# Six-layer local-attention kernel: the first loads in another order with semaphores of their own, and the local stage's first buffers filled while the causal stage ends

## The reference, cut to what matters

```python
mod = (_silu(c) @ wmod).reshape(8, 6, 1, -1)
sa, ca, ga, sb, cb, gb = (mod[:, i] for i in range(6))      # ga, gb kept at least 0.25 from zero
h = _layernorm(x) * (1 + ca) + sa
x = x + ga * attn(h, Wq, Wk, Wv, Wo, bo)                    # 16 heads of 64, causal
h = _layernorm(x) * (1 + cb) + sb
x = x + gb * ffn(h)                                         # what follows, six times over
...
for i in range(6):
    x = attn_layer(shift_tokens(x), Wqkv[i], q_scale[i], k_scale[i], Wo[i]) + x    # windows of 32 tokens, rotary
    x = ffn_layer(shift_tokens(x), ln_g[i], ln_b[i], W1[i], b1[i], W2[i], b2[i]) + x
```

## Time and profile before

| what | us |
|---|---|
| median of 3 runs | 4071.61 |
| lowest and highest of the 3 | 4069.26, 4075.61 |
| time of the profiled execution | 4063.49 |
| span of the profiled execution (first to last record) | 4061.4 |
| TensorE busy in it | 3807.5 |
| VectorE, ScalarE, GpSimd busy | 3026.9, 2350.1, 2311.4 |

### The profile page before, as it was taken

The page is one execution under the profiler, slowest core; times in us unless marked ns, Lnnn a source line. Parts: engine busy times, 40 slices in busy tenths (PEclk is TensorE's granted clock), DMA queues, the critical chain, the costliest instruction groups (busy, mean ns, idle before and its releaser), DMA issues.

```text
span 4061.4 us, 162148 instructions
## 1 busy us (share of the span) xinstructions
PE 3807.5 (94%) x72308; PEld 2145.7 (53%) x72308; DVE 3026.9 (75%) x3509; ACT 2350.1 (58%) x2850; POOL 2311.4 (57%) x1892
## 2 busy tenths in 40 slices
PE   7999999779999999999999999999899999999996
PEld 3555555445555555554555555555555555555553
DVE  6878777667777777776777777777777777777774
ACT  4555565546565656565656565565566566656553
POOL 3554454366565656665666656665556565666661
PEclk9999999889999999999999999999999999999998
DMA  1000000144444444443444444444444444454442
GB/s 54 4 4 4 4 4 4 38 103 98 108 98 105 102 113 108 110 107 90 107 114 100 104 97 113 107 104 98 101 114 98 106 99 105 104 115 96 110 103 80
DMA packets 162062, 348.69 MB, mean 86 GB/s; under 512 B 32606, under 2 KB 41948, under 8 KB 155100
## 3 DMA queue, kind: packets, MB, share of 16 engines
q1 hardware_dynamic: 161372, 338.32, 35.7%
HBM read 24.24 MB, written 4.19 MB: 7 GB/s over the span
## 4 chain that ended last, share of the span: by engine, by line
PE 45%; issue 2%; DMA 2%; DVE 2%; ACT 1%; SPq 1%; ACTq 0%; DVEq 0%
PE psB L632 22%; PE psA L632 17%; DMA vev<-vo 2%; PE psB L710 2%; PE psA L684 2%; PE psB L684 1%; ACT pb L937 1%; PE psA L710 1%; SPq L452 1%; SPq L468 0%; DMA kf<-h 0%; SPq L470 0%; DVE h L1163 0%; DVE wvtl L1115 0%; DVE ts L1155 0%
## 5 line engine op out<-in xcount | busy, mean ns | idle before, releaser
L1263 POOL TENSOR_TENSOR sq<-sq 128x512 f32<-128x512 f32 x384 | 490.2, 1295 | 469.5 <-ACT sq L907 468.9
L1258 POOL TENSOR_TENSOR h<-h,ts 128x512 f32<-128x512 f32 x384 | 489.9, 1276 | 210.5 <-DVE ts L1155 210.5
L1239 POOL TENSOR_TENSOR pt<-wk,pt 128x1024 f16<-128x1024 f32 (+3 forms) x256 | 367.7, 1454 | 399.8 <-DVE pt L1096 322.1
L1259 POOL TENSOR_TENSOR h<-h,ts 128x512 f32<-128x512 f32 x384 | 490.6, 1277 | 0.0
L907 ACT ACTIVATE sq<-psA 128x1024 f32<-128x1024 f32 x240 | 245.8, 1024 | 168.1 <-PE psA L632 168.1
L1147 DVE TENSOR_TENSOR h<-psA,t_rot 128x1024 f32<-128x1024 f32 x240 | 293.0, 1221 | 46.0 <-ACT sq L907 20.3
L632 PE MATMUL psB<-vev,ptb 64*32 64x65 f32 x9216 | 244.5, 225 | 55.9 <-ACT pb L937 36.9
L1155 DVE TENSOR_TENSOR ts<-psA,t_rot 128x1024 f32<-128x1024 f32 x240 | 291.4, 1214 | 3.1 <-POOL h L1259 3.1
L632 PEld LDWEIGHTS psB<-vev,ptb 64*32 64x32 f32 x9216 | 194.4, 106 | 173.1 <-issue 98.4
L1273 POOL TENSOR_SCALAR f_a<-f_a 128x512 f32<-128x512 f32 x48 | 31.2, 650 | 404.5 <-DVE f_a L1203 404.5
L1163 DVE TENSOR_TENSOR h<-h,psB 128x1024 f32<-128x1024 f32 x192 | 229.5, 1217 | 42.3 <-PE psB L632 40.2
(11 more groups left out here) (332 smaller groups left out, 10640.6 us busy)
## 6 DMA issues: line engine op xcount, KB each, us to landing
qf<-h SPq DMA_DIRECT2D x768, 136.0 KB
kf<-h SPq DMA_DIRECT2D x768, 136.0 KB
vev<-vo SPq DMA_DIRECT2D x192, 260.0 KB, 4.1
vev<-vo SPq DMA_DIRECT2D x192, 227.5 KB, 4.5
stage<-wqk SPq DMA_DIRECT2D x12, 512.0 KB, 4.8
stage<-wvl SPq DMA_DIRECT2D x12, 256.0 KB, 5.4
stage<-wof SPq DMA_DIRECT2D x6, 512.0 KB, 4.6
xb<-xt SPq DMA_DIRECT2D x8, 256.0 KB, 7.2
```

Source lines behind the costliest of these rows:

```text
L1239: e.tensor_tensor(pt[g][pr][:, :, 1, o:o + w], wk[(slot_of(s)[0] - 1) % SLOTS][:, :, 0:w], pt[g][pr][:, :, 0, o:o + w], ALU.subtract).then ...
L1258: e.tensor_tensor(halves_of(h, 0), halves_of(h, 0), t[1], ALU.subtract)
L1259: e.tensor_tensor(halves_of(h, 1), halves_of(h, 1), t[0], ALU.add).then_inc(ended["ad"])
L1263: e.tensor_tensor(sqb[c][:, 0, :], sqb[c][:, 0, :], sqb[c][:, 1, :], ALU.add).then_inc(ended["qa"])
```

## The change

The loads at the start are issued in another order and count on more semaphores (`s_ct`, `s_first`, `s_wa` for each weight). ScalarE's exponential waits for `ct` alone. The splitting of the causal weights is cut into three steps that stand at places inside batch 0, the first product with q and k weights waits for two of the three, and VectorE's work on the masks stands behind batch 0's layernorm, with a semaphore `s_masks`. TensorE waits for x of batch 0 only, and for the rest at batch 1.

The early buffers are allocated in another order, so that `stage`, `t_tab` and `xs0` lie over `ot0` (last read by `c_op` of batch 6), `wq` and `wvt` over `w16`, `xs1` and `n_s` over `h160` and `ht0`, and `t_rot` over `pt1`. SyncE loads `stage` and `t_tab` after `c_op` of batch 6. Each engine does its first local steps inside the end of the causal walk, and TensorE waits for the four PSUM tiles to come free instead of for `s_xk`.

```diff
+        ot0 = sb("ot0", [128, 8, S], F32, early)
+        w16 = [sb(f"w16{z}", [128, 3, 1024], F16, early) for z in "hl"]
+        h160 = [sb(f"h160{z}", [128, S], F16, early) for z in "hl"]
+        ht0 = sb("ht0", [128, S], F32, early)
+        pt1 = [sb(f"pt1{i}", [128, 2, 2, 8 * 160], F16, early) for i in range(2)]
...
+        stage = sb("stage", [128, 1536])
+        t_tab = sb("t_tab", [128, 4, S])
+        xs0 = [sb(f"xs0{z}", [128, S], F16) for z in "hl"]
...
         def sync(e):
-            for o, i in ((t_mats[:, :], mats), (st_masks[:, :], masks), (st_left[:, :], left), (t_vec[:, :], vecs),
-                         (t_ct[:, 0, :], ct)):
+            e.dma_start(t_ct[:, 0, :], ct).then_inc(s_ct, 16)
+            e.dma_start(t_wmod[:, :], wmod).then_inc(s_wm, 16)
+            e.dma_start(t_mats[:, :], mats).then_inc(s_first, 16)
+            e.dma_start(xb[:, 0, 0:S], xt[0]).then_inc(s_first, 16)
...
+                    if b == NB - 2:
+                        e.wait_ge(*full(("c_op", b)))
+                        heads_of(e, 0, 0)
+                        e.dma_start(flat(t_tab), tab).then_inc(s_tab, 16)
+                        e.dma_start(t_scl[:, :, :], scl).then_inc(s_tab, 16)
             for n in range(2):
                 e.wait_ge(s_xk[n], 4)
-            e.dma_start(flat(t_tab), tab).then_inc(s_tab, 16)
-            e.dma_start(t_scl[:, :, :], scl).then_inc(s_tab, 16)
-            heads_of(e, 0, 0)
             feed_of(e, 0)
...
         def tensor(e):
-            e.wait_ge(s_x, 128)
+            e.wait_ge(s_first, 32)
...
+                    elif b == 1:
+                        e.wait_ge(s_x, 16 * (NB - 1))
...
-                    e.wait_ge(s_w16, 3)
+                    e.wait_ge(s_w16, 2)
...
-            for n in range(2):
-                e.wait_ge(s_xk[n], 4)
+            for c in range(2):
+                for i in range(2):
+                    e.wait_ge(s_free[c][i], max(n for a, z, n in use.values() if (a, z) == (c, i)) + 1)
             local_tensor(e)
...
         def scalar(e):
+            e.wait_ge(s_ct, 16)
+            e.activation(t_ct[:, 1, :], t_ct[:, 0, :], ACT.Exp, scale=-1.0).then_inc(s_actc)
             e.wait_ge(s_pads, 1)
...
+                if s == last_of("c_v", "c_qk", "c_sc"):
+                    e.wait_ge(s_xk[0], 1)
+                    local_scalar(e, scalar_walk[:2])
+                if s == last_of("c_ot"):
+                    for at in ((1, 1, 0), (1, 1, 1)):
+                        e.wait_ge(*full(("c_va", NB - 1) + at))
+                    local_scalar(e, scalar_walk[2:3])
             for n in range(2):
                 e.wait_ge(s_xk[n], 4)
-            local_scalar(e)
+            local_scalar(e, scalar_walk[3:])
...
         def vector(e):
+                        if b == 0:
+                            weight_low(1)
+                            e.wait_ge(s_const, 48)
+                            e.tensor_copy(t_masks[:, :], st_masks[:, :])
+                            e.tensor_copy(flat(t_sel), st_left[:, :]).then_inc(s_masks)
+                            weight_low(2)
...
+                if s == last_of("c_va"):
+                    e.wait_ge(*full(last_of("c_v", "c_qk")))
+                    weights_low(e, -2)
             local_vector(e)
...
         def gpsimd(e):
+            local_gpsimd(e, gpsimd_walk[:1])
             for n in range(2):
                 e.wait_ge(s_xk[n], 4)
-            local_gpsimd(e)
+            local_gpsimd(e, gpsimd_walk[1:])
```

More of the change, by code:

```diff
@@ L267, in program @@
         oq = [sb(f"oq{n}", [128, 4, 256], F32, early) for n in range(2)]
-        ot = [sb(f"ot{n}", [128, 8, S], F32, early) for n in range(2)]
         wbig = flat(ot[0])[:, 0:3 * 1024]
@@ L276, in program @@
         early.close()
+        stage = sb("stage", [128, 1536])
+        t_tab = sb("t_tab", [128, 4, S])
+        xs0 = [sb(f"xs0{z}", [128, S], F16) for z in "hl"]
         wq = [sb(f"wq{z}", [128, 2, 2, 2, 2, 128], F16) for z in "hl"]
         wvt = [sb(f"wvt{z}", [128, 2, 2, 256], F16) for z in "hl"]
-        stage = sb("stage", [128, 1536])
-        xs = [[sb(f"xs{n}{z}", [128, S], F16) for z in "hl"] for n in range(2)]
+        xs = [xs0, [sb(f"xs1{z}", [128, S], F16) for z in "hl"]]
+        n_s = sb("n_s", [128, S])
+        t_rot = sb("t_rot", [128, 2, 2, 2, S])
         wo2 = [sb(f"wo{z}", [128, 8, 128], F16) for z in "hl"]
@@ L287, in program @@
         b1s = sb("b1s", [128, 6])
-        t_tab = sb("t_tab", [128, 4, S])
-        t_rot = sb("t_rot", [128, 2, 2, 2, S])
         hb = [sb(f"h{n}", [128, 2, WK]) for n in range(HN)]
@@ L296, in program @@
         sqb = [sb(f"sq{n}", [128, 2, S]) for n in range(4)]
-        n_s, n_r, n_a = (sb("n_" + x, [128, S]) for x in ("s", "r", "a"))
+        n_r, n_a = (sb("n_" + x, [128, S]) for x in "ra")
         vo = [sb(f"vo{n}", [128, 8, 4, 65]) for n in range(2)]
@@ L321, in program @@
         s_full, s_free = [sems(f"s_full{c}", 2) for c in range(2)], [sems(f"s_free{c}", 2) for c in range(2)]
-        s_const, s_x, s_wa, s_wo, s_wm, s_w1, s_w2, s_tab, s_stage, s_x1r = (
-            sem("s_" + n) for n in ("const", "x", "wa", "wo", "wm", "w1", "w2", "tab", "stage", "x1r"))
+        s_wa = sems("s_wa", 3)
+        s_const, s_first, s_ct, s_x, s_wo, s_wm, s_w1, s_w2, s_tab, s_stage, s_x1r = (
+            sem("s_" + n) for n in ("const", "first", "ct", "x", "wo", "wm", "w1", "w2", "tab", "stage", "x1r"))
         s_dm = sems("s_dm", 4)
@@ L328, in program @@
         s_out = sem("s_out")
-        s_pads, s_chain, s_silu, s_mod, s_actc, s_z = (sem("s_" + n) for n in ("pads", "chain", "silu", "mod", "actc", "z"))
+        s_masks, s_pads, s_chain, s_silu, s_mod, s_actc, s_z = (sem("s_" + n) for n in ("masks", "pads", "chain", "silu", "mod", "actc", "z"))
         s_lnq, s_lnl, s_lnr, s_lnn = (sems("s_" + n, 2) for n in ("lnq", "lnl", "lnr", "lnn"))
@@ L357, in both, with last_of @@
             return tile(key).rearrange("p (x s) -> p x s", x=2)[:, :, 0:w]
+        def last_of(*kinds):
+            return [s for s in causal if s[0] in kinds][-1]
         def full(key):
@@ L417, in sync @@
         def sync(e):
[L418 to L426 removed]
+            e.dma_start(t_ct[:, 0, :], ct).then_inc(s_ct, 16)
+            e.dma_start(t_wmod[:, :], wmod).then_inc(s_wm, 16)
+            e.dma_start(t_mats[:, :], mats).then_inc(s_first, 16)
+            e.dma_start(xb[:, 0, 0:S], xt[0]).then_inc(s_first, 16)
+            e.dma_start(t_vec[:, :], vecs).then_inc(s_const, 16)
+            for n, w in enumerate((wqa, wka)):
+                e.dma_start(wbig[:, 1024 * n:1024 * n + 1024], w).then_inc(s_wa[n], 16)
+            for o, i in ((st_masks[:, :], masks), (st_left[:, :], left)):
+                e.dma_start(o, i).then_inc(s_const, 16)
+            e.dma_start(wbig[:, 2048:3072], wva).then_inc(s_wa[2], 16)
+            for b in range(1, NB):
                 e.dma_start(xb[:, b, 0:S], xt[b]).then_inc(s_x, 16)
@@ L866, in weights_high, with local_scalar @@
             e.activation(flat(wvt[0][:, half]), stage[:, 1024:1536], ACT.Copy, scale=WS).then_inc(ended["wh"])
-        def local_scalar(e):
+        def local_scalar(e, steps):
             tables = "natural_log_exp_and_others"
-            for s in scalar_walk:
+            for s in steps:
                 kind, v = s[:2]
@@ L1031, in vector, with weight_low @@
                 chained(e.tensor_tensor(g, t_ct[:, 0, :], t_ct[:, 2, :], ALU.mult))
-            for i in range(3):
+            def weight_low(i):
                 e.wait_ge(s_w16h, i + 1)
@@ L1125, in local_vector @@
             e.memset(vev.rearrange("p c r d -> p (c r d)"), 0.0).then_inc(s_init)
-            for s in vector_walk:
+            for s in vector_walk[1:]:
                 kind, v = s[:2]
```

34 lines of the change are left out of this document (16 added, 18 removed).

## The result

| what | before | changed |
|---|---|---|
| median, us | 4070.12 (6 runs, 4065.47 to 4075.61) | 4044.64 (6 runs, 4040.67 to 4057.8) |
| time of the profiled execution, us | 4063.49 | 4041.46 |
| span of the profiled execution, us | 4061.4 | 4039.5 |

The ratio is 0.9943 [0.9926, 0.996]: faster by 0.57%. By the medians 25.5 us went, by the profiled executions 22.0; forecast were 21.2 us, a time of 4050.4 and a span of 4040.2.

The account below looks back on a forecast made before the run. TensorE was taken as busy nine tenths or more except at the start and the stage step, where serial chains left it idle. Gains 9.1 + 12.1 = 21.2 us gave 4071.6 - 21.2 = 4050.4 us, range 4042 to 4062.

Parts of the forecast that it names:

- The start: Kernel start: reordered loads begin layernorm 10.3 us earlier, less 1.2 for a `w16l` on the path; net 9.1 us.
- upper bound of 9.9 us: Start term's spread, 7.0 to 9.9 us, by the two ends of the landing of `wmod` and x.
- The step: Causal to local stage: early loads and preparation start the first local product at 793.7 instead of 805.82, 12.1 us earlier.
- the cover ahead of `wu`: End of causal stage: ScalarE's eight `t_rot` go into 8.66 us of idle time, leaving 3.7 us.
- So the whole stage shifts.: Causal stage: nothing later is tied to absolute time, so the start's 9.1 us carries through it.
- bound of 3 us for the local stretch: Sign of error: first local product to the end differing by more than 3 us from before.
- more than forecast: Rival: TensorE runs fewer products slowly and VectorE's small steps close up; 2 to 5 us more, 4046; chance 0.06.
- The start gives less: Rival at the start: loads compete, x of batch 0 takes 7.2 us; start gives 7.0, time 4052.5; chance 0.12.
- The step gives less: Rival at the step: some wait keeps the old order, only the start's gain is left; 4062.5; chance 0.09.
- Given back in the local stage: Rival: pipeline starting in another state loses some of the 21 us in first local batches; 4062 to 4071; chance 0.07.
- Slower: Rival: GpSimd and VectorE collide, 0.85 us on each of 48 local batches, 41 us, 4091; chance 0.03.

Follow-up runs that it names:

- idle products: Changed kernel plus 34 products that nothing reads in TensorE's idle time of the start (7 before the `mod` product, 27 in batch 0's layernorm); one execution, 4033.02 us.
- The step further: Changed kernel with VectorE's clearings moved inside the causal walk's end and ScalarE's first square ahead of its wait for the last x; 4043.44 us, ratio 0.9934.

## Why the prediction was right

**The start (forecast 9.1, measured 9.2).** Layernorm 10.42 earlier against 10.3, less 1.21 for the `w16l` on the path against 1.2. Inside it two sizes were off and cancelled. I had silu ready at 4.3 and `wmod` in at 3.9. `ct` landed in 1.8 us and the exponential started at 2.54, so with the 1.08 us behind it silu was ready at 3.6; `wmod` took 3.3 and ended the wait at 4.53, so that the forecast 4.5 was right by luck. (The Trainium skill, DMA: Bandwidth & Descriptors, Anatomy of one DMA, gave an estimate of 2.9 us for this transfer; the measured 3.3 is longer. The page's fit is for DMAs issued by GpSimd, and this one is SyncE's.) The upper bound of 9.9 us for this term does not follow from the prediction's own rows: with silu ready at 4.3 the term is at most 9.3. Old order and new waits show that what I costed as one thing is two, 3.9 and 6.5 us.

**The step (forecast 12.1, measured 12.14).** The loads were in long before, the early instructions went into the idle times named, the cover ahead of `wu` was 3.77 us against 3.7, and VectorE's clearing ended last. Experiments split it 6.3, 4.65 and 1.2. The clearing as the bound is confirmed by moving it away with the square: the gap fell to 0.09.

**"So the whole stage shifts."** Here the working was incomplete. Every wait kept its place, but 1.4 us were lost where TensorE's clock was lower for some microseconds in this execution. The local stage gave 1.6 us more, and on the way its lead over the kernel before, taken at each of VectorE's instructions, wandered between 14.2 and 23.4 us. Of one such rise, from 18.9 to 21.6, the windows show what went with it; before:

```profile
2906.00:2930.00 24.00, 19.99 (x333) 10.84 (x332) 10.43 (x13) 13.53 (x21) 7.99 (x8) 0.79 0.29 66
```

and the changed kernel at its place in the program:

```profile
2887.00:2911.00 24.00, 19.99 (x366) 10.61 (x371) 12.35 (x16) 15.94 (x23) 9.17 (x9) 0.93 0.33 74
```

In both TensorE is busy for 19.99 us, but at a granted clock of 0.79 it gets through 333 products, at 0.93 through 366. My bound of 3 us for the local stretch held here by luck: the same kernel again took 3258.4, 2.8 from the kernel before, and other kernels with the same instructions there lie up to 10.5 from it.

**The medians (25.5 against 21.2).** 4.3 us are inside the ratio's interval (16 to 30 us). I take them for this wandering; that is argued from the table of stretches and from the second comparison, where the same kernel gained 21.9 us by the medians, and not shown by a run of its own. By its number alone 4044.6 lies nearer to the rival "more than forecast" (4046) than to the forecast.

**The rivals.** *The start gives less:* no, no x ended a wait. *The step gives less:* no. *Given back in the local stage:* the medians show no loss (25.5 and 21.9 us); of the traces the stretch is within its own scatter, and a few microseconds could not be seen in it. *More than forecast:* not at the start, where TensorE ran at its lower level as before and the q and k products stand 0.43 apart in both kernels; bought with idle products, the upper level is worth 1.3 to 2.5 us at the second `qk1l`, and whether it lasts is not shown. *Slower:* GpSimd's `n_a`, against the earlier trace rows (duration in ns, min/median/max, first and last start):

```profile
L1314 POOL TENSOR_SCALAR n_a<-n_a x96: 617/618/1473, 801.4 to 3946.2; 128x512 f32<-128x512 f32 x96
```

and the timeline of VectorE and GpSimd at its longest one:

```profile
801.20 1.24 DVE L1158 SCALAR_TENSOR_TENSOR wql<-stage,wqh 128x1024 f16<-128x1024 f32 x1 [3.37 <-ACT wvth L901]
801.44 1.47 POOL L1314 TENSOR_SCALAR n_a<-n_a 128x512 f32<-128x512 f32 x1
```

One of the steps took 1473 ns, in the fill, beside a `wql`: the same single collision as before, though the stage begins 20 us earlier. In all 13 traces exactly one of the 96 is over 700 ns, and it is this one (1469 to 1477 ns), with stages that begin anywhere from 780.1 to 805.8: the phase between the two engines does not hang on when the stage begins. The Trainium skill (SBUF — State Buffer, SBUF: two separate sides) states that these two engines share ports that are locked for a whole instruction; these rows agree.

**Best version.** The step further has the lowest ratio, 0.9934 [0.9912, 0.9956], but it overlaps the changed kernel's 0.9943 and 0.9947. Only its gap, 2.8 us shorter, speaks for it.

## What to carry to other kernels

At a step between two stages, list per engine what stands between the last result of one and the first of the other, and for each instruction what it truly needs; loads come first (6.3 of 12.1 us here), then the engines' own preparation into idle times that a trace shows with their length (4.65), then waits that ask for more than they need (1.2 here, and 6.5 at the start, more than the 3.9 that the order of the loads gave). Keep the cover's width beside each such move.

Where an edit is worth less than half a per cent, compare marks set by waits in two traces: here they returned within 0.1 us, while a single time or an untouched stretch varied by up to 20 us.

## What the hardware showed that was not expected

- TensorE's granted clock fell in the middle of a busy stage, at other places in each execution: 0.66 from 165 to 170 us in the changed kernel, 1.00 in the same part of the program before, and the same pair of products took 2.02 us in the one and 1.08 in the other and in the changed kernel's second trace. Unedited stretches of 755 and 3255 us varied by 8 and 20 us; the first goes with the time at 1.2 GHz (10.2 to 34.1 us), the second does not.
- The granted clock in the windows view is 1.00 from 20 to 26 us in the changed kernel, while its products stand 0.43 us apart as at 1.2 GHz: at the start durations tell the level, and that figure does not.
- Seven f16 products in 3.17 us directly ahead of the first real work left it at the lower level (2.06 us for a pair that takes 1.08 at the upper one); 27 more, 22 of them in 5.58 us, were followed by products 0.22 us apart instead of 0.43. From 28.41 us on they were 0.43 apart again, at a granted clock of 0.50.
- A chain made late by 1.2 us on ScalarE came out 2.1 us late: a TensorE product pair behind the longer wait took 2.04 us instead of 1.10.
